# Attention layer of a four-layer graph kernel: one graph per step, scores in 32-row strips, maximum taken from PSUM and subtracted into SBUF

## The chip, the core and the metric

The kernel runs on one core of one Trainium2 chip. The metric is the device time of one execution in microseconds (us); the kernel before takes 859.26 us, the median of three runs (859.25 to 859.69). Engines are named TensorE (PE; its weight loads are PEld), VectorE (DVE), ScalarE (ACT), GpSimd (POOL) and SyncE (SP, here only transfers).

## What is computed

64 graphs of 128 nodes with 128 features go through four layers; each ends in `x = layernorm(layer(x) + x)`. Layer 2 (the third; they are counted from 0) is the one that changes: attention of 8 heads of width 16 in each graph, under the graph's adjacency.

```python
q = heads(x @ Wq.T + bq)
k = heads(x @ Wk.T + bk)
v = heads(x @ Wv.T + bv)
scores = jnp.einsum('bhnd,bhmd->bhnm', q, k) / math.sqrt(D)
...
```

Scores of absent edges are masked, a softmax runs over each row, its weights are multiplied with `v`, the heads are put side by side and multiplied with `Wo.T`, and `bo` is added. Layers 0 and 1 (a relational convolution and an attention of one head) come before it, layer 3 (additive attention, 8 heads) after it.

## The kernel before

`X` holds all 64 graphs in SBUF, 16 batches of `G` = 4 graphs. One layer runs over all batches before the next starts, and `later_layers` writes out the order of layers 1, 2 and 3 for each of PE, ACT and DVE; the few steps at a seam between layers are woven by hand (`layer2(BATCHES)` with `layer3(-1)`, for example). Every engine has its own program in this fixed order, and semaphores tie them; nothing is reordered by a scheduler. `need(eng, sem, v)` waits only if `v` is above zero.

Layer 2 works in units `u` of four heads of one graph, 8 units per batch, 128 in all. For one unit, on the engines:

- PE `layer2`: the mask (-1e30 for absent edges, bfloat16) goes into `bank[u % 2]` by a matmul with the identity (L1052), and the scores are added by one float32 matmul of 512 columns (L1054). Its moving operand `kexp` holds `k` once for each head with the other heads' rows at zero, so that the contraction over all 128 rows gives one head. POOL writes `kexp` in 8 operations per batch (L547, L550).
- DVE takes the negative maximum of each head from PSUM (L820, 512 elements per partition). ACT takes the exponential head by head, with that maximum as bias and the sum accumulated (L692, four operations and four reads of the accumulator). DVE takes the reciprocal (L851) and scales the weights in SBUF (L853).
- PE transposes the four 128x128 weights (L946, by `transposes`) into bank 2 or 3, ACT copies them (`copy_pT`, L667), PE multiplies them with `v` (`p_times_v`, L1039): four matmuls with 32 stationary columns, two heads in one group of 32 PSUM partitions, two groups. ACT copies the result (`copy_oT`, L676) and PE applies `Wo` (L1077).
- Once per batch come the transposes of the next `x`, the products for `k`, `q` and `v`, the adds of `bo` and `x`, the statistics and the norm.

Two units' scores stand in two banks in turn: while DVE and ACT work on one, PE fills the other. On PE a unit's scores stand ahead of the transposes of unit u-2 and the products of unit u-3. A float32 matmul appears as two matmul records (two passes) in the trace, a transpose as one.

`l3_weights` is DVE's preparation between layers 0 and 1, behind the flag (L316) that all engines branch on.

Of the kernel before, what the change touches and what calls it, by code (L numbers as in the profile page):

```python
# [11 lines left out]
F32 = mybir.dt.float32  # L12
BF16 = mybir.dt.bfloat16
# [35 lines left out]

def real(b):  # L50
    return not isinstance(b, int) or 0 <= b < BATCHES
# [10 lines left out]
def later_layers(eng, layer1, layer2, layer3, last):  # L62


    every_batch(eng, layer1, before=True, after=1)
    layer2(-1, 1, -1)
    layer1(BATCHES + 1, 1, BATCHES // 2)
    every_batch(eng, layer2)
    for u in range(UNITS):
        layer2(BATCHES, 0, BATCHES // 2, (u,))  # L70
        layer3(-1, 1, -1, (u,))
    layer2(BATCHES + 1, 1, BATCHES // 2)
    every_batch(eng, layer3, after=last)


def build(nc, t, out):
    ctx = ExitStack()
    with ctx:
# [10 lines left out]
        bank = [ctx.enter_context(nc.psum_tensor(f"bank{i}", [128, 512], F32)) for i in range(8)]  # L89
# [24 lines left out]
        qk_bias = sb("qk_bias", [128, 3])  # L114
        bv_row = sb("bv_row", [128, D])
# [54 lines left out]
        kT = sb("kT", [128, W])  # L170
        kexp = sb("kexp", [128, 2 * HEADS * W])
        adj = kexp[:].bitcast(I32)


        v2 = work
# [3 lines left out]
        den = [sb(f"den{i}", [128, HQ]) for i in range(4)]  # L179
        rd = [sb(f"rd{i}", [128, HQ]) for i in range(4)]  # L180
# [17 lines left out]
        def heads_of(mask, b, g):  # L198

            return mask[:, bass.ts(G * b + g, N)].unsqueeze(1).broadcast_to([128, HQ, N])  # L200

# [23 lines left out]
        add(oT_w[:], nat["L2_gnn_Wo"])  # L225
        add(bil[:], w1T[:], a12w[:], a12w_at)
        add(wa1[:], w1T[:], a_cols[:, 0:1].broadcast_to([128, 128]), w1_at)
# [32 lines left out]
        gsum = kexp[:, 0:GRAPHS * D]  # L260
# [57 lines left out]
        def general_dve(dve):  # L318
            def body(dve):
# [10 lines left out]
                def step(i, g, loop, r):  # L330
# [11 lines left out]
                    else:  # L342
                        nc.vector.tensor_tensor(ghg, bank[2][:], gbias, ALU.add).then_inc(sem("G_hg"), 1)
# [31 lines left out]
        def l3_weights(dve):  # L375
            dve.wait_ge(sem("params"), sems["n_params"])

# [127 lines left out]
        def _(pool):  # L505
# [31 lines left out]
            def layer1(b, s, turn):  # L537
                if isinstance(b, int) and b == BATCHES - 1:
                    layer2(-1, 1, -1)
                norm_pool(pool, 1, b, s, turn)  # L540

            def layer2(b, s, turn):
                if real(b + 1):
                    pool.wait_ge(sem("L2_k"), b + 2)
                    need(pool, sem("L2_s_mm"), UNITS * b)

                    nc.gpsimd.tensor_tensor(kexp[:, cols((1 - s) * HEADS, W)], kT[:],  # L547
                                            headmask[:, 0:1].broadcast_to([128, W]), ALU.mult)
                    for h in range(1, HEADS):
                        last = nc.gpsimd.tensor_scalar(kexp[:, cols((1 - s) * HEADS + h, W)], kT[:],  # L550
                                                       headmask[:, h:h + 1], 1.0, ALU.mult, ALU.mult)
                    last.then_inc(sem("L2_kexp"), 1)
                if real(b - 2):
                    norm_pool(pool, 2, b - 2, s, turn - 1)

            every_batch(pool, layer1)
            every_batch(pool, layer2, after=2)

            def layer3(b, s, turn):
                for u in range(UNITS):  # L560
                    if real(b):
# [14 lines left out]
        def _(act):  # L576
# [6 lines left out]
            for dst, src in ((nat["L0_gnn_W_loop"], t["L0_gnn_W_loop"][:, :]), (nat["L0_gnn_Wg_loop"], t["L0_gnn_Wg_loop"][:, :]),  # L583
# [6 lines left out]
                      (bv_row[:], row(t["L2_gnn_bv"], D)), (bo_row[:], row(t["L2_gnn_bo"], D)),  # L590
# [32 lines left out]
            def layer1(b, s, turn):  # L623
# [7 lines left out]
                if real(b):  # L631
# [3 lines left out]
                    nc.scalar.activation(uT[s], bank[1][:], ACT.Identity, bias=wa1[:, 0:1]).then_inc(sem("L1_uT"), 1)  # L635
# [508 lines left out]
```

## Time and profile before

| | |
|---|---|
| median of 3 runs | 859.26 us |
| the profiled execution | 859.89 us |
| its span (first to last instruction) | 858.2 us |
| PE busy | 781.1 us (91%) |
| DVE busy | 687.8 us (80%) |
| ACT busy | 642.2 us (75%) |
| POOL busy | 445.8 us (52%) |
| layer 2, first to last maximum (L820) | 229.1 to 572.1 us |
| layer 3, first mask matmul to the end | 583.8 to 858.2 us |

Busy time is the union of an engine's instructions; matmuls overlap in the pipeline, so PE's share says that it has work in flight, not that it runs at its peak. The span is the time from the first instruction to the last; about 1 us lies around it. Window rows further down give the busy time of each engine in a stretch, timeline rows give starts and durations.

### The profile page before, as it was taken

How to read it: one execution, taken by the hardware profiler on the slowest of the kernel's cores; microseconds unless marked ns; L12 is line 12 of the kernel's file. 1: busy time of each engine (PE TensorE's matmuls, PEld its weight loads, DVE VectorE, ACT ScalarE, POOL GpSimd, SP SyncE). 2: the span in 40 equal slices, each digit the busy share in tenths (PEclk: the TensorE clock that was granted, in tenths of full speed). 3: DMA queues.
4: the chain of work that ended last, by engine and by line, in shares of the span. 5: the costliest groups of instructions: out<-in, count | busy, mean ns of one | idle time of the engine just before them, and what ended most of it. 6: DMA issues, size and time to landing. Idle time of an engine off the chain costs nothing.

```text
span 858.2 us, 19137 instructions
## 1 busy us (share of the span) xinstructions
PE 781.1 (91%) x6059; PEld 527.3 (61%) x6059; DVE 687.8 (80%) x1919; ACT 642.2 (75%) x2116; POOL 445.8 (52%) x598
## 2 busy tenths in 40 slices
PE   3998899996699999999999999997999999999993
PEld 2776677775366666565666666555666666666652
DVE  3899288887577888888888888867899999999994
ACT  1544477777287777777777777776999999999993
POOL 4477233333533444444444444416567767767765
PEclk9999899999799999999999999998999999999998
DMA  8700000000000000000000000000000000000001
GB/s 247 205 2 1 2 1 2 1 2 1 1 1 1 2 1 2 2 1 2 2 2 1 1 1 2 2 1 1 2 14 14 27 15 14 27 14 14 26 14 38
DMA packets 28901, 15.09 MB, mean 18 GB/s; under 512 B 1792, under 2 KB 28800, under 8 KB 28800
## 3 DMA queue, kind: packets, MB, share of 16 engines
q1 hardware_dynamic: 25344, 12.59, 4.9%
q10 hardware_dynamic: 3456, 1.27, 0.6%
q8 instruction: 50, 0.82, 0.4%
q14 instruction: 51, 0.42, 0.2%
HBM read 9.65 MB, written 4.19 MB: 16 GB/s over the span
## 4 chain that ended last, share of the span: by engine, by line
PE 62%; DVE 17%; ACT 8%; issue 8%; POOL 2%; DMA 1%; DVEq 1%; POOLq 0%; ACTq 0%
PE bank L946 14%; PE bank L1054 12%; PE bank L1039 11%; PE bank L1052 5%; ACT loopm L640 3%; PE bank L1091 2%; DVE nmx L918 2%; DVE P L898 2%; PE bank L1094 2%; PE bank L1107 2%; DVE pT L804 2%; PE bank L1077 2%; PE bank L1012 2%; PE bank L1092 2%; PE bank L1006 2%
## 5 line engine op out<-in xcount | busy, mean ns | idle before, releaser
L692 ACT ACTIVATE P<-bank,nmx 128x128 f32<-128x128 f32 x512 | 181.3, 366 | 80.7 <-DVE nmx L820 80.5
L564 POOL TENSOR_TENSOR P<-P,nmx 128x512 f32<-128x512 f32 x128 | 133.2, 1041 | 80.5 <-DVE nmx L918 78.5
L946 PE MATMUL bank<-identf,P 128*128 128x128 f32 x1024 | 155.5, 274 | 1.6 <-DVE P L853 1.6
L667 ACT COPY pT<-bank 128x512 f32<-128x512 f32 x256 | 151.5, 593 | 0.4 <-PE bank L946 0.4
L820 DVE TENSOR_REDUCE nmx<-bank 128x4 f32<-128x512 f32 x128 | 88.3, 690 | 64.1 <-PE bank L1054 62.2
L459 POOL TENSOR_TENSOR ln<-ln,neghalf 128x4 f32<-128x4 f32 x64 | 66.2, 1034 | 138.6 <-DVE ln L495 138.6
L1054 PE MATMUL bank<-kexp,hg 128*128 128x512 f32 x256 | 132.3, 598 | 0.0
L946 PEld LDWEIGHTS bank<-identf,P 128*128 128x128 f32 x1024 | 113.9, 141 | 24.0 <-DVE P L853 14.2
L465 POOL TENSOR_SCALAR X<-yb,ln 128x128 f32<-128x128 f32 x256 | 119.4, 481 | 9.2 <-issue 9.2
L853 DVE TENSOR_TENSOR P<-P,rd 128x512 f32<-128x512 f32 x128 | 109.9, 859 | 4.4
L547 POOL TENSOR_TENSOR kexp<-kT,headmask 128x512 f32<-128x512 f32 x16 | 16.7, 1041 | 178.6 <-DVE kT L829 178.6
L898 DVE TENSOR_TENSOR P<-bank,t 128x512 f32<-128x512 f32 x128 | 87.5, 683 | 21.0 <-ACT t L707 20.8
L692 ACT ACTIVATION_READ_ACCUMULATOR P<-bank,nmx 128x1 f32 x512 | 103.9, 203 | 0.0
L550 POOL TENSOR_SCALAR kexp<-kT,headmask 128x512 f32<-128x512 f32 x112 | 102.8, 938 | 0.0
L707 ACT ACTIVATE t<-bank 128x512 f32<-128x512 f32 x128 | 77.7, 607 | 21.1 <-PE bank L1094 20.9
L918 DVE TENSOR_REDUCE nmx<-P 128x4 f32<-128x512 f32 x128 | 85.7, 670 | 0.8
L1039 PE MATMUL bank<-pT,work 128*32 128x128 f32 x1024 | 81.6, 279 | 1.7 <-ACT oT L676 0.9
L711 ACT ACTIVATE P<-P 128x512 f32<-128x512 f32 x128 | 80.9, 632 | 2.2 <-POOL P L564 2.2
L1039 PEld LDWEIGHTS bank<-pT,work 128*32 128x32 f32 x1024 | 47.4, 109 | 23.4 <-issue 21.0
L486 DVE BATCH_NORM_STATS2 bn<-yb 128x6 f32<-128x128 f32 x256 | 60.8, 281 | 1.2
L1094 PEld LDWEIGHTS bank<-eT,sel 128*128 128x128 bf16 x512 | 39.8, 99 | 31.1 <-issue 1.6
L1039 PE MATMUL bank<-pT,vx 128*32 128x128 f32 x1024 | 54.5, 285 | 2.0 <-ACT pT L667 1.8
(158 smaller groups left out, 1504.3 us busy)
## 6 DMA issues: line engine op xcount, KB each, us to landing
X<-in_x SPq DMA_DIRECT2D x16, 256.0 KB, 5.4
kexp<-in_adj SPq DMA_DIRECT2D x16, 256.0 KB, 5.3
out<-X SPq DMA_DIRECT2D x16, 256.0 KB, 2.3
nat_all<-in_L_gnn_W ACTq DMA_DIRECT2D x2, 64.0 KB, 4.1
w<-in_L_gnn_W ACTq DMA_DIRECT2D x2, 64.0 KB, 4.6
nat_all<-in_L_gnn_W_loop ACTq DMA_DIRECT2D x1, 64.0 KB, 2.7
nat_all<-in_L_gnn_Wg_loop ACTq DMA_DIRECT2D x1, 64.0 KB, 3.3
hg_bias<-in_L_gnn_b_loop ACTq DMA_DIRECT2D x1, 64.0 KB, 5.1
```

What stands on the lines that cost most here:

```text
L465: last = nc.gpsimd.tensor_scalar(x_of(b)[:, cols(g)], yb[s][:, cols(g)], ln[s][:, g:g + 1], ln[s][:, 2 * G + g:2 * G + g + 1], ALU.add, AL ...
L550: last = nc.gpsimd.tensor_scalar(kexp[:, cols((1 - s) * HEADS + h, W)], kT[:], headmask[:, h:h + 1], 1.0, ALU.mult, ALU.mult)
L564: nc.gpsimd.tensor_tensor(v3(P[u % 4][:], HQ), v3(P[u % 4][:], HQ), nmx[u % 4][:].unsqueeze(2).broadcast_to([128, HQ, N]), ALU.add)\
L667: nc.scalar.copy(pT[uu % 2][:], bank[2 + uu % 2][:]).then_inc(sem(f"L{L}_pT"), 1)
L692: last = nc.scalar.activation(P[u % 4][:, cols(j)], bank[u % 2][:, cols(j)], ACT.Exp, bias=nmx[u % 4][:, j:j + 1], accum_out=den[u % 4][:, ...
L820: nc.vector.tensor_reduce(nmx[u % 4][:], v3(bank[u % 2][:], HQ), AX.X, ALU.max, negate=True)\
L853: nc.vector.tensor_tensor(v3(P[uu % 4][:], HQ), v3(P[uu % 4][:], HQ), rd[uu % 4][:].unsqueeze(2).broadcast_to([128, HQ, N]), ALU.mult)\
L898: nc.vector.tensor_tensor(P[u % 4][:], bank[u % 2][:], t3[u % 2][:], ALU.max)\
L918: nc.vector.tensor_reduce(nmx[u % 4][:], v3(P[u % 4][:], HQ), AX.X, ALU.max, negate=True)\
L946: last = nc.tensor.transpose(dst[:, cols(i)], src[:, cols(i)], identf[:])
L1039: last = mm(bank[6][row:row + HP, cols(col)], (v2 if L == 2 else vx)[ss][:, cols(HEADS * g + h, HP)], pT[uu % 2][:, cols(j)], start=start, ...
L1054: mm(bank[u % 2][:], qT[s][:, cols(g)], kh, start=False, stop=True).then_inc(sem("L2_s_mm"), 1)
```

## The change

Layer 2 is written anew as a step `t` per graph (64 steps, and 16 that drain), with all 8 heads at once:

- `pair[0]` is banks 0 and 1 as one PSUM tensor of 1024 columns, `pair[1]` banks 2 and 3. One graph's scores take the whole of `pair[0]`, and there is no second buffer for them: PE's mask matmuls of graph t wait for `L2_less_max` of graph t-1.
- `kexp` and POOL's writes of it are gone. ACT writes `kk`: for even and odd heads, `k` with the other half's rows at zero. A strip is a matmul whose operands are 32 rows of `qT` and `kk` (two heads), 256 columns wide. Strips 0 and 1 go to banks 0 and 1, then come the 8 transposes of graph t-2, then strips 2 and 3, again to banks 0 and 1.
- DVE takes the maximum over 1024 columns from PSUM and then adds its negative to the scores, from PSUM into `P2` in SBUF. ACT takes one exponential of 1024 columns there. The sum of a row is no longer accumulated: `v` is held as `vx`, 32 columns a head with a column of ones, so the product gives the sum as well. The 8 products of a graph go to four groups of 32 partitions (`HP * (h % 4)`).
- Their result is transposed back (2 transposes per graph), scaled by the reciprocal of the sum into `on` (DVE), per batch transposed again (`onT`), multiplied with `Wo`, with `bo` added by a bfloat16 matmul of three parts. `bv` and the parts of `bo` are prepared in `l3_weights` and one more `prep` product.
- ACT copies `xT` and writes `k` and `q`. The norm is split over POOL's steps. The first two units of layer 3 wait for the last residual of layer 2 (`L2_y_done`).

```diff
     every_batch(eng, layer1, before=True, after=1)
-    layer2(-1, 1, -1)
+    for t in range(-4, 0):
+        layer2(t)
     layer1(BATCHES + 1, 1, BATCHES // 2)
-    every_batch(eng, layer2)
+    for t in range(GRAPHS):
+        layer2(t)
     for u in range(UNITS):
-        layer2(BATCHES, 0, BATCHES // 2, (u,))
+        layer2(GRAPHS + u)
         layer3(-1, 1, -1, (u,))
...
         def l3_weights(dve):
             dve.wait_ge(sem("params"), sems["n_params"])
+            dve.wait_ge(sem("pool_ready"), 1)
+            nc.vector.tensor_reduce(evenodd[:], headmask[:].rearrange("p (a b) -> p b a", b=2), AX.X, ALU.add)\
+              .then_inc(sem("kmask_set"), 1)
+            nc.vector.memset(bo3[:], 0.0).then_inc(sem("bo_set"), 1)
...
+            nc.vector.tensor_tensor(bo2[:], bvo[:], bo_row[:], ALU.add).then_inc(sem("bo_set"), 1)
+            for part in range(3):
...
+                nc.vector.tensor_copy(bo_part[:], bo2[:]).then_inc(sem("bo_set"), 1)
...
+                nc.vector.tensor_copy(v3(bo3[at, :], G), bo_part[at, :].unsqueeze(1).broadcast_to([1, G, D]))
+                nc.vector.tensor_tensor(bo2[:], bo2[:], bo_part[:], ALU.subtract).then_inc(sem("bo_set"), 1)
```

ScalarE, per step: `k` of the next batch, the copy of the transposed weights, the exponential, the copy of the product:

```diff
+                if j == 1 and real(b + 1):
+                    act.wait_ge(sem("L2_k_mm"), b + 2)
...
+                    for e in range(2):
+                        last = nc.scalar.activation(k[:, e], v3(bank[5], G), ACT.Identity, bias=bk2[:, e:e + 1],
+                                                    scale=evenodd[:, e:e + 1])
...
+                if graph(t - 2):
+                    act.wait_ge(sem("L2_pT_mm"), t - 1)
+                    need(act, sem("L2_pv_mm"), t - 3)
+                    nc.scalar.copy(pT2[t % 2], pair[1][:]).then_inc(sem("L2_pT"), 1)
+                if graph(t - 1):
+                    act.wait_ge(sem("L2_less_max"), t)
+                    p = P2[(t - 1) % 3]
+                    nc.scalar.activation(p, p, ACT.Exp).then_inc(sem("L2_exp"), 1)
+                if graph(t - 3):
...
+                    nc.scalar.copy(oT[(t - 3) % 2][:], bank[6][:, 0:2 * N]).then_inc(sem("L2_oT"), 1)
```

VectorE:

```diff
+                if graph(g):
+                    dve.wait_ge(sem("L2_out_mm"), g + 1)
+                    nc.vector.reciprocal(rd3[g % 2][:], o[:, :, HD]).then_inc(sem("L2_rden"), 1)
...
+                if graph(t):
+                    dve.wait_ge(sem("L2_s_mm"), 2 * (t + 1))
+                    need(dve, sem("L2_pT_mm"), t - 2)
+                    nc.vector.tensor_reduce(nmx2[t % 2][:], v3(pair[0][:], HEADS), AX.X, ALU.max, negate=True)\
+                      .then_inc(sem("L2_max"), 1)
+                    dve.wait_ge(sem("L2_max"), t + 1)
+                    nc.vector.tensor_tensor(v3(P2[t % 3], HEADS), v3(pair[0][:], HEADS),
+                                            nmx2[t % 2][:].unsqueeze(2).broadcast_to([128, HEADS, N]), ALU.add)\
+                      .then_inc(sem("L2_less_max"), 1)
```

TensorE, up to the last strips:

```diff
+                def strips(first):
+                    for i in range(first, first + 2):
+                        rows = slice(HP * i, HP * i + HP)
+                        last = mm(bank[i % 2][:, cols(i // 2, 2 * N)], qT[s][rows, cols(j)], kk[s][rows, cols(j, 2 * N)],
+                                  start=False, stop=i >= 2)
...
+                if graph(t):
...
+                    need(pe, sem("L2_less_max"), t)
+                    for i in range(2):
+                        mm(bank[i], identb[:], heads_of(mask2, b, j), start=True, stop=False)
+                    strips(0)
+                if graph(t - 2):
+                    pe.wait_ge(sem("L2_exp"), t - 1)
+                    need_or(pe, sem("L2_pT"), t - 2, sem("L1_xw"), BATCHES)
+                    for i in range(2):
+                        last = transposes(bank[2 + i], P2[(t - 2) % 3][:, cols(i, W)], HQ)
+                    last.then_inc(sem("L2_pT_mm"), 1)
+                if graph(t):
+                    pe.wait_ge(sem("L2_s01_mm"), 2 * (t + 1))
+                    strips(2)
```

TensorE, layer 3:

```diff
                         need(pe, sem("L3_leaky"), U - 1)
...
+                        if U < 2:
+                            pe.wait_ge(sem("L2_y_done"), BATCHES)
```

On PE in the middle of layer 2, one graph was two units; these rows are one unit and the start of the next, before (`bank`, `kexp`, `hg`: scores from `kexp` and `qT`; `identf,P`: transposes; `pT,work`: products with `v`):

```order
L1052 MATMUL bank<-mask,identb 128x512 [waits L2_exp]
L1054 MATMUL bank<-kexp,hg 128x512
L1077 MATMUL bank<-oT_w,oT 128x128 [waits L2_oT]
L946 MATMUL bank<-identf,P 128x128 [waits L2_pT,L2_p]
L946 MATMUL bank<-identf,P 128x128 x3
L1039 MATMUL bank<-pT,work 32x128 [waits L2_pT]
L1039 MATMUL bank<-pT,work 32x128 x3
```

The same place after the change, one whole graph with the batch's transposes of `x` and products for `v` (`arena,hg`: strips of `kk` and `qT`; `identf,arena`: transposes of `P2`; `arena,vx`: products with `v`):

```order
L1064 MATMUL pair<-mask,identb 128x512 [waits L2_less_max,L2_q,L2_k]
L1055 MATMUL pair<-arena,hg 128x256 x2
L979 MATMUL pair<-identf,arena 128x128 [waits L2_pT,L2_exp]
L979 MATMUL pair<-identf,arena 128x128 x7
L1055 MATMUL pair<-arena,hg 128x256 [waits L2_s01_mm]
L1055 MATMUL pair<-arena,hg 128x256
L1082 MATMUL bank<-arena,vx 32x128 [waits L2_oT,L2_pT]
L1082 MATMUL bank<-arena,vx 32x128 x7
L979 MATMUL bank<-identf,oT 128x128 [waits L2_on,L2_oT]
L979 MATMUL bank<-identf,X 128x128 [waits L2_xT,L2_y_done,L1_norm_done]
L1099 MATMUL bank<-vT_w,xT 128x128 [waits L2_q]
```

The first score matmul waited for the exponential of two units earlier, and now waits for the subtraction of the graph just before; the transposes stand between the strips.

On DVE the same stretch before, a unit's maximum, a copy for the batch, and the reciprocal and scaling of the unit ahead:

```order
L820 TENSOR_REDUCE nmx<-bank 128x4 [waits L2_exp,L2_s_mm]
L825 COPY xT<-bank 128x512 [waits L2_v_mm,L2_xT_mm]
L851 RECIPROCAL rd<-den 128x4 [waits L2_exp]
L853 TENSOR_TENSOR P<-P,rd 128x512 [waits L2_rden]
```

And after, one graph, with the batch's copy of `onT` (`hg`):

```order
L869 RECIPROCAL rd<-bank 128x8 [waits L2_out_mm]
L878 COPY hg<-bank 128x512 [waits L2_o_mm,L2_onT_mm]
L887 TENSOR_TENSOR arena<-bank,rd 128x128 [waits L2_rden]
L893 TENSOR_REDUCE nmx<-pair 128x8 [waits L2_pT_mm,L2_s_mm]
L896 TENSOR_TENSOR arena<-pair,nmx 128x1024 [waits L2_max]
```

All four rows stood there twice per graph (the copy once per batch). The scaling moved from the weights to the product, and a pass of the width of the scores came in behind the maximum.

On DVE between the flag and the first operation of layer 1 these now stand ahead of the old preparation (`bo` stands for `bo2` and `bo3`):

```order
L403 TENSOR_REDUCE evenodd<-headmask 128x2 [waits pool_ready,params]
L407 TENSOR_SCALAR bk<-evenodd,qk_bias 128x2 [waits kmask_set]
L413 CAST bo_part<-bo 128x128 [waits bo_set]
L415 COPY bo<-bo_part 1x512 [waits bo_set]
L416 TENSOR_TENSOR bo<-bo,bo_part 128x128
L419 TENSOR_TENSOR a_prod<-nat_all,a_row 128x128 x2
```

The last three of the new ones come three times; `a_prod` was first before.

## Rows read from the trace of the kernel before

**Rows 1.** The page: its span, and the granted clock in 40 slices.

```profile
span 858.2 us, 19137 instructions
...
PEclk9999899999799999999999999998999999999998
```

**Rows 2.** Windows, layers 2 and 3: busy PE, PEld, DVE, ACT, POOL; then the granted clock.

```profile
583.80:858.20 274.40, 248.97 (x2672) 165.95 (x2672) 239.65 (x673) 239.35 (x508) 185.51 (x215) 0.98 0.06 17
229.10:572.10 343.00, 339.95 (x2238) 205.20 (x2238) 274.70 (x614) 269.74 (x1217) 151.35 (x192) 1.00 0.01 1
```

**Rows 3.** Line L820: ns minimum/median/maximum, first and last start in us.

```profile
L820 DVE TENSOR_REDUCE nmx<-bank x128: 676/692/694, 229.1 to 572.1; 128x4 f32<-128x512 f32 x128
```

**Rows 4.** Waits in layer 2: who waited for whom, us in total, times, longest.

```profile
DVE nmx L820 <- PE bank L1054: 61.8, 94, 3.1
...
PEld bank L946 <- DVE P L853: 14.2, 20, 2.4
```

**Rows 5.** Timeline of PE through one unit of layer 2: start, duration, instructions.

```profile
429.46 0.60 PE L946 MATMUL bank<-identf,P 128*128 128x128 f32 x4
429.99 0.64 PE L1039 MATMUL bank<-pT,work 128*32 128x128 f32 x8
430.56 0.39 PE L1052 MATMUL bank<-mask,identb 128*128 128x512 bf16 x1
430.79 0.59 PE L1054 MATMUL bank<-kexp,hg 128*128 128x512 f32 x1
```

**Rows 6.** Timeline of layer 2: DVE to DVE, DVE to PE, PE to DVE.

```profile
233.26 0.17 DVE L851 RECIPROCAL rd<-den 128x4 f32<-128x4 f32 x1
...
233.46 0.69 DVE L853 TENSOR_TENSOR P<-P,rd 128x512 f32<-128x512 f32 x1
...
234.20 0.33 PE L946 MATMUL bank<-identf,P 128*128 128x128 f32 x1 [1.55 <-DVE P L853]
...
433.83 1.02 PE L1054 MATMUL bank<-kexp,hg 128*128 128x512 f32 x2
...
434.89 0.69 DVE L820 TENSOR_REDUCE nmx<-bank 128x4 f32<-128x512 f32 x1 [0.76 <-PE bank L1054]
```

**Rows 7.** Timeline of layer 3: the products with `v`, four heads in four groups.

```profile
701.69 0.43 PE L1039 MATMUL bank<-pT,vx 128*32 128x128 f32 x8
```

**Rows 8.** Groups by line: count, busy us, mean ns, idle time before them.

```profile
L763 DVE TENSOR_TENSOR vals<-bank,hg 128x256 f32<-128x256 f32 x32 | 11.9, 414 | 7.5 <-ACT hg L609 7.5
L898 DVE TENSOR_TENSOR P<-bank,t 128x512 f32<-128x512 f32 x128 | 87.5, 683 | 21.0 <-ACT t L707 20.8
L667 ACT COPY pT<-bank 128x512 f32<-128x512 f32 x256 | 151.5, 593 | 0.4 <-PE bank L946 0.4
L711 ACT ACTIVATE P<-P 128x512 f32<-128x512 f32 x128 | 80.9, 632 | 2.2 <-POOL P L564 2.2
L748 DVE COPY bias<-bias_part 1x256 bf16<-1x256 bf16 x6 | 1.3, 297 | 0.1
L379 DVE TENSOR_TENSOR a_prod<-nat_all,a_row 128x128 f32<-128x128 f32 x2 | 0.5, 277 | 0.0
```

**Rows 9.** Timeline, layer 0 to layer 1: the end of `l3_weights` and DVE's next operation.

```profile
90.26 0.16 DVE L387 COPY wh_w<-a_sum 128x8 f32<-128x8 f32 x1
...
91.43 0.69 DVE L795 COPY xT<-bank 128x512 f32<-128x512 f32 x1 [1.01 <-PE bank L946]
```

**Rows 10.** Timeline, layer 1 to layer 2.

```profile
220.02 1.16 PE L1069 MATMUL bank<-vT_w,xT 128*128 128x128 f32 x8
...
221.97 1.00 DVE L784 SCALAR_TENSOR_TENSOR elu<-pT,elu 128x512 f32<-128x512 f32 x1 [2.01 <-ACT elu L630]
...
226.78 0.59 PE L1052 MATMUL bank<-mask,identb 128*128 128x512 bf16 x1 [5.60 <-POOL kexp L550]
```

**Rows 11.** Timeline, layer 2 to layer 3: the last maximum and the first mask of layer 3.

```profile
572.05 0.69 DVE L820 TENSOR_REDUCE nmx<-bank 128x4 f32<-128x512 f32 x1 [0.35 <-PE bank L1054]
...
583.79 0.61 PE L1091 MATMUL bank<-mask,identb 128*128 128x512 bf16 x1 [0.68 <-ACT eT L702]
```

More of the change, by code:

```diff
@@ L47, in need_or, with graph @@
         eng.wait_ge(sem, value)
+HEAD_AT = (0, 1, 4, 5, 2, 3, 6, 7)
+def graph(t):
+    return 0 <= t < GRAPHS
 def real(b):
@@ L87, in sem @@
             return sems[name]
-        bank = [ctx.enter_context(nc.psum_tensor(f"bank{i}", [128, 512], F32)) for i in range(8)]
+        pair = [ctx.enter_context(nc.psum_tensor(f"pair{i}", [128, 1024], F32)) for i in range(2)]
+        bank = [pair[i // 2][:, i % 2 * 512:i % 2 * 512 + 512] for i in range(4)]
+        bank += [ctx.enter_context(nc.psum_tensor(f"bank{i}", [128, 512], F32))[:] for i in range(4, 8)]
         def cols(i, n=D):
@@ L169, in build @@
         qT = [uT[s] for s in range(2)]
[L170 to L175, printed above, removed]
+        arena = sb("arena", [128, 16 * W])
+        adj = arena[:].bitcast(I32)
+        P2 = [arena[:, cols(i, 2 * W)] for i in range(3)]
+        pT2 = [arena[:, cols(3 + i, 2 * W)] for i in range(2)]
+        kk = [arena[:, cols(5 + i, 2 * W)] for i in range(2)]
+        on = [arena[:, cols(14 + i, W)] for i in range(2)]
+        onT = y2[0]
         vx = [sb(f"vx{s}", [128, G * HEADS * HP]) for s in range(2)]
@@ L200, in heads_of, with out_bank @@
             return mask[:, bass.ts(G * b + g, N)].unsqueeze(1).broadcast_to([128, HQ, N])
+        def out_bank(b):
+            return bank[4] if b < BATCHES - 2 else bank[1]
         prep = []
@@ L537, in layer1, with layer2 @@
             def layer1(b, s, turn):
-                if isinstance(b, int) and b == BATCHES - 1:
-                    layer2(-1, 1, -1)
                 norm_pool(pool, 1, b, s, turn)
[L542 to L554, printed above, removed]
+            def layer2(t):
+                b, j = t // G - 3, t % G
+                if j == 3 and real(b):
+                    norm_pow(pool, 2, b, b % 2, b // 2)
+                    norm_scale(2, b, b % 2, (0, 1))
+                if j == 0 and real(b - 1):
+                    norm_scale(2, b - 1, (b - 1) % 2, (2, 3))
             every_batch(pool, layer1)
-            every_batch(pool, layer2, after=2)
+            for t in range(GRAPHS + UNITS):
+                layer2(t)
             def layer3(b, s, turn):
                 for u in range(UNITS):
+                    if b == 0:
+                        layer2(GRAPHS + UNITS + u)
                     if real(b):
@@ L1082, in layer3 @@
+                        row, col = HP * j, 2 * (g % 2) + hq
+                        last = mm(bank[6][row:row + HP, cols(col)], vx[ss][:, cols(HEADS * g + h, HP)],
+                                  pT[uu % 2][:, cols(j)], start=True, stop=True)
+                    last.then_inc(sem(f"L{L}_pv_mm"), 1)
             def layer3(b, s, turn, units=range(UNITS)):
```

314 lines of the change are left out of this document (156 added, 158 removed).

## The prediction

> **What bounds the kernel now.** First the page: the span is 858.2 us, and the granted clock is high nearly throughout, with dips near the seams between layers [rows 1]. Then the windows: in layer 2, PE has work in flight in 339.95 of 343.00 us at clock 1.00, while DVE is busy 274.70 and ACT 269.74 [rows 2]. The waits agree: DVE waits 61.8 us for PE's scores, PE waits 14.2 us for DVE's scaled weights, nearly all of it at the start, and almost nothing else [rows 4]. So layer 2 is bound by PE's stream. Its period is (572.1 - 229.1) / 127 = 2.70 us per unit, 5.40 per graph [rows 3]. Whoever shortens PE's stream and keeps two score buffers gains; this change shortens the stream but gives the second buffer up. So the question is no longer how much work PE has, but how long one turn of the loop mask, strips, maximum, subtraction, next mask takes.
>
> **The step of PE.** Unit rows give starts, and the differences are what an item costs in a full stream [rows 5]. Four transposes and the change to the 32-column products: 429.99 - 429.46 = 0.53. A transpose in the stream is 0.11 (0.60 for four, of which 0.27 is the pipeline of the last), so 0.09 is a pause at the change of shape. The eight passes of the products and the pause behind them take 430.56 - 429.99 = 0.57. A mask matmul takes 0.23, and a float32 matmul of 512 columns 0.86 in two passes of 0.43 (its two records span 1.02, 0.17 beyond the stream [rows 6]), so a pass of 256 columns takes 0.21.
>
> Do matmuls in different parts of the array overlap? For column groups, yes: eight passes over two groups span 0.64 [rows 5], eight over four groups 0.43 [rows 7]; four rounds became two. For row groups no row shows it. Bounds for a pair of strips: fully side by side 2 x 0.21 = 0.43, in a row 0.86. I take side by side, since the column rows are the nearest and the two strips write different banks. The first weights after a pause are not hidden: eight passes of a 128-column float32 product span 1.16 after idle time [rows 10], where 7 x 0.11 + 0.28 = 1.05 would do; so 0.10 for each pair of strips, and 0.05 before transposes (0.33 for the first one after a wait [rows 6], 0.28 in the stream).
>
> From the first mask to the end of the last strip: masks 0.44; pause 0.09; strips 0 and 1 0.54; pause 0.09; eight transposes 0.05 + 0.87; pause 0.09; strips 2 and 3 0.54, and 0.17 until the result is there. Sum 2.88.
>
> The rows show a pause of 0.09 at each change of shape. The Trainium skill (TensorEngine Tiling, Key Properties) says that changing the tiling mode drains the engine; the trace agrees, for column shapes. For row tiles it gives (TensorE: Matmul & The Clock Gate, Measured speedup vs the span model) 3.07 times for four of 512 columns, the only figure for what no row here shows; by it a pair would be nearly side by side, as in my sum.
>
> **The step of DVE.** A two-operand pass from PSUM takes 414 ns for 256 columns and 683 for 512 [rows 8], so 1.05 ns a column; 1024 take 1.22. The maximum takes 0.69 for 512 [rows 3], by the same slope 1.23. DVE starts 0.04 after the scores' end (433.83 + 1.02 to 434.89), 0.03 lie between dependent operations, and PE starts 0.05 after DVE's end (233.46 + 0.69 to 234.20) [rows 6]. Together 0.04 + 1.23 + 0.03 + 1.22 + 0.05 = 2.57.
>
> **The loop** takes 2.88 + 2.57 = 5.45 us per graph. What else must fit beside it? PE behind the last strip: products 0.09 + 0.46, two transposes 0.36 with pause, and per step one of: `x` transposes and `v` 1.33, `k` and `onT` 1.30, `q` 0.86, `bo` and `Wo` 1.10. That ends by 2.71 + 0.91 + 1.33 = 4.95, under 5.45: hidden, with 0.5 to spare. DVE's reciprocal, scaling and one copy (0.2 + 0.3 + 0.7, and two statistics 0.5) lie beside PE's 2.88. ACT has a copy of 1024 (0.59 + 0.42), an exponential (0.63 + 0.42), a copy of 0.40 and at most two passes of 0.7: 3.9 us. All are covered; each costs nothing as long as the loop stays above 4.95. POOL's `kexp` goes, but it was not on the path except at the first batch.
>
> So PE's load per graph does fall (about 4.7 against 5.40), and none of that is seen, because the loop's 5.45 takes its place. 63 x 5.45 = 343.4 against 343.0: **+0.4**. The rows show DVE's two passes as 2.57 of 5.45. The Trainium skill (TensorEngine Tiling, PSUM Bottleneck) warns that tiling speeds up the engine and not the way out of PSUM; by it, as by the rows, the gain of the strips stays unpaid here.
>
> **The seams.** Layer 0 to 1: 12 more operations on DVE, of 0.15 to 0.3 each (a_prod 277 ns, a one-row copy of 256 elements 297 ns, so some 0.5 for 512 [rows 8]), three rounds of a chain of three, about 1.0 each, and 0.6 ahead of them. DVE stood 1.01 us between its last preparation and the copy [rows 9], and part of that is the branch on the flag, which stays; so nearly all of 3.6 shows: **+3.5** (bounds 2.5 and 5).
>
> Layer 1 to 2: PE stood 5.60 us for `kexp` [rows 10]. ACT's `k` (2 x 0.7) comes instead, then `q` must wait for it since both use bank 5. In rows 10 `v` starts at 220.02 behind `q`, so `k`'s product is there at about 219.1; 219.1 + 1.4 + 1.0 for `q` + 0.7 on ACT gives the first mask at about 222.2 instead of 226.78. But DVE's tail of layer 1 now hides nothing: ACT begins that tail behind `q`, at 222.2 instead of 220.7, and DVE's part starts at 223.5 instead of 221.97. It takes 3.2 instead of 4.1 without POOL beside it (1.00 for a pass that takes 0.69 elsewhere). So the first maximum comes at 226.8 instead of 229.1: **-2.3**. PE then waits some 3 us for the first subtraction, so the next steps run at the lower clock: **+1.5** (0 to 3).
>
> Layer 2 to 3: before, 583.79 - 572.05 = 11.7 us from last maximum to first mask of layer 3 [rows 11]. Now: maximum and subtraction 2.5; exponential behind a copy 2.6; transposes 1.1; copy 1.05; products 0.8; copy 0.45; back transposes 0.35; `Wo` of batch 14 with its residual 2.0; scaling 0.3; `onT` 0.6 and copy 0.75; `bo` and `Wo` 1.3; residual 0.7, for which layer 3's first mask waits. Sum 14.5: **+2.8** (0 to 5). Statistics and norm of the last batch now lie in layer 3's first units: **+0.5**.
>
> Sum: 0.4 + 3.5 - 2.3 + 1.5 + 2.8 + 0.5 = +6.4, so a span of 864.6. The profiled execution's own time (859.89) lies 0.6 above the median and its span 1.1 below the median; from the median, **865.7 us**.
>
> **Rivals.**
> 1. *The strips don't overlap.* For it: no row shows row groups side by side. Against: rows 5 and 7 show column groups so, and the banks differ. Each pair costs 0.43 more: 63 x 0.86 = +54, 920 us. If only their weight loads queue up, about half a pass per pair, 63 x 0.22 = +14, 880.
> 2. *The other side: the strips need no pause.* If the array takes row strips between full matmuls without a pause and loads their weights ahead, three pauses (0.27) and the exposed loads (0.25) go: the loop is 4.93, and PE's own stream, 4.4 to 4.7, nearly binds too. 63 x (4.93 - 5.45) = -33: 833 us. It decides for faster from a loop under 5.35, that is if 0.10 goes per graph. For it: half of PE's changes of shape in the old stream cost nothing visible (bfloat16 mask to float32 scores), but those are all full-sized. Against: every change to or from a part of the array costs 0.09 or more in rows 5.
> 3. *The early weights only.* One exposed load is hidden or one pass is shorter than I take it: loop 5.3, -9.5, 856 us.
> 4. *The clock.* PE stands 0.5 us per step; layer 3 stands more (busy 248.97 of 274.40) and keeps 0.98 [rows 2]. So I give it little; at the lower clock the loop would gain over 2 us.
>
> **Chances.** Forecast with its neighbourhood (858 to 874) 0.52; rival 1 in full 0.11, in part 0.11; rival 2 0.13; rival 3 0.11; clock 0.02. The range should leave out full rival 1 and the clock and reaches to the others: 832 to 884. Measurement tells 0.2% (1.7 us) from no change. Faster (below 857.5): rivals 2 and 3 and a little of the neighbourhood, 0.29; same 0.09; slower 0.62.
>
> **What would show it.** Start to start of L893 (maximum) should be 5.45 in mid-stage; the strips' four records should start in two close pairs, 0.21 apart, some 0.1 late after masks and transposes (in rival 1, four starts 0.21 apart). L893 and L896 should take 1.22 to 1.23 each. PE's mask L1064 should wait for DVE L896 in nearly every step, about 0.5 us; if it doesn't, PE's stream binds and the working of the pauses is wrong. The first L893 should stand 1 us or so later than 229.1 (+3.5 - 2.3), the first mask of layer 3 at about 588. The prediction fails if a pair of strips takes clearly other than 0.54, or if DVE or ACT holds the loop at a place that I call covered.

## The result, and the profile after

The kernel after takes **885.10 us** (median of four runs, 881.33 to 888.53) beside 859.44 of the kernel before (859.25 to 859.69). The ratio is 1.0297, with a 95% interval of 1.0252 to 1.0342: slower by 3%. The prediction had the sign and the loop that sets the step of layer 2, but a quarter of the size: +6.4 us where +25.7 came, and 885.1 lies just outside its range of 832 to 884. What failed most is its term for the lower clock of TensorE: it had +1.5 us, and layer 2 lost 10.8.

The page of the profiled execution (886.5 us), its busy line, the granted clock in 40 slices and the three groups that make the loop:

```profile
span 884.7 us, 18573 instructions
...
PE 769.3 (87%) x6525; PEld 519.9 (59%) x6525; DVE 636.1 (72%) x1754; ACT 554.1 (63%) x1141; POOL 325.3 (37%) x470
...
PEclk9999899998659999999999999979999999999998
...
L893 DVE TENSOR_REDUCE nmx<-pair 128x8 f32<-128x1024 f32 x64 | 78.4, 1225 | 135.4 <-PE pair L1055 135.4
...
L896 DVE TENSOR_TENSOR arena<-pair,nmx 128x1024 f32<-128x1024 f32 x64 | 78.4, 1224 | 2.2
...
L1064 PE MATMUL pair<-mask,identb 128*128 128x512 bf16 x128 | 40.7, 401 | 40.4 <-DVE arena L896 39.4
```

Every engine has less to do than before, and the program is longer: DVE stands 135.4 us before the maximum, waiting for the strips, and PE stands 40.4 us before the mask, nearly all of it for DVE's subtraction. That is a loop of two engines in turn. The clock row has a dip to 6 and 5 in slices 11 and 12 (7 and 9 in rows 1 of the kernel before), where layer 2 begins, and one to 7 in slice 27, where it ends (before, 8 in slice 28).

Windows of the kernel after (stretch, its length; busy PE, PEld, DVE, ACT, POOL; granted clock, DMA share, GB/s). The last row is the middle of layer 2, to be held against the second of [rows 2]:

```profile
240.10:264.00 23.90, 21.60 (x100) 12.28 (x100) 8.35 (x9) 7.92 (x10) 0.00 (x0) 0.50 0.00 1
264.00:281.00 17.00, 13.62 (x117) 7.07 (x114) 8.57 (x12) 8.82 (x12) 0.00 (x0) 1.00 0.01 1
281.00:284.50 3.50, 3.50 (x24) 2.48 (x28) 0.49 (x1) 1.68 (x2) 0.00 (x0) 0.51 0.00 0
...
584.80:595.10 10.30, 10.27 (x52) 7.25 (x53) 4.83 (x15) 2.34 (x3) 2.74 (x5) 0.50 0.01 3
286.00:584.00 298.00, 267.07 (x2326) 162.27 (x2324) 190.31 (x382) 154.23 (x214) 32.86 (x60) 1.00 0.01 1
```

PE had work in flight in 339.95 of 343.00 us; now in 267.07 of 298.00, at full clock. It stands a tenth of the time. And 37.7 us of layer 2 and its end (23.9 + 3.5 + 10.3) ran at 0.50, the lower level of 1.2 GHz.

The waits of the kernel after from 286 to 584 us (engine, line, waited for: us in total, times, longest), which answer to [rows 4]:

```profile
DVE nmx L893 <- PE pair L1055: 103.1, 54, 2.6
...
PEld pair L1064 <- DVE arena L896: 38.2, 41, 1.6
...
PE pair L1064 <- DVE arena L896: 30.0, 53, 1.2
```

**Where the 26.5 us of span went.** Five marks in both timelines divide it:

| stretch | before | after | more | forecast |
|---|---|---|---|---|
| start to the first maximum of layer 2 | 229.11 | 231.46 | +2.4 | +1.2 |
| first to last maximum | 342.94 | 358.67 | +15.7 | +1.9 |
| last maximum to the first mask of layer 3 | 11.74 | 19.17 | +7.4 | +2.8 |
| that mask to the end | 274.37 | 275.39 | +1.0 | +0.5 |

The step of the loop, taken from the starts of L893 in mid-stage, is 5.50, 5.50, 5.51 and 5.58 within a batch, 5.523 on average. 63 steps of it are 347.9, that is +5.0 against before; the other 10.8 of the 15.7 are steps that ran at the lower clock (up to 7.92 us each).

### The profile page after: what moved, and what is told of

It reads as the page before. It is cut to its first block, busy times and chain, and to the rows that moved or that the text cites. A ratio compares the mean times of both kernels' runs of the same rounds, so it can differ in the third digit from the quotient of the medians.

```text
span 884.7 us, 18573 instructions
## 1 busy us (share of the span) xinstructions
PE 769.3 (87%) x6525; PEld 519.9 (59%) x6525; DVE 636.1 (72%) x1754; ACT 554.1 (63%) x1141; POOL 325.3 (37%) x470
## 4 chain that ended last, share of the span: by engine, by line
PE 47%; DVE 33%; issue 8%; ACT 7%; POOL 2%; DVEq 1%; DMA 1%; POOLq 1%; ACTq 0%
PE pair L979 11%; PE pair L1055 10%; DVE arena L896 9%; DVE nmx L893 9%; PE pair L1064 4%; PE bank L979 4%; ACT loopm L675 3%; PE bank L1145 2%; PE pair L1160 2%; DVE nmx L951 2%; DVE P L931 2%; PE pair L1163 2%; PE bank L1045 2%; PE pair L1161 2%; DVE pT L853 2%
## 5 line engine op out<-in xcount | busy, mean ns | idle before, releaser
L893 DVE TENSOR_REDUCE nmx<-pair 128x8 f32<-128x1024 f32 x64 | 78.4, 1225 | 135.4 <-PE pair L1055 135.4
L736 ACT COPY arena<-pair 128x1024 f32<-128x1024 f32 x64 | 64.8, 1012 | 172.1 <-PE pair L979 172.1
L931 DVE TENSOR_TENSOR P<-pair,t 128x512 f32<-128x512 f32 x128 | 87.5, 684 | 22.4 <-ACT t L756 20.5
L1055 PE MATMUL pair<-arena,hg 32*128 32x256 f32 x512 | 95.2, 449 | 0.2
L756 ACT ACTIVATE t<-pair 128x512 f32<-128x512 f32 x128 | 77.4, 605 | 22.9 <-PE pair L1163 22.6
L896 DVE TENSOR_TENSOR arena<-pair,nmx 128x1024 f32<-128x1024 f32 x64 | 78.4, 1224 | 2.2
L979 PE MATMUL pair<-identf,P 128*128 128x128 f32 x512 | 78.2, 275 | 0.0
L979 PE MATMUL pair<-identf,arena 128*128 128x128 f32 x520 | 75.9, 292 | 1.7 <-DVE arena L887 1.0
L1064 PE MATMUL pair<-mask,identb 128*128 128x512 bf16 x128 | 40.7, 401 | 40.4 <-DVE arena L896 39.4
L702 ACT COPY pT<-pair 128x512 f32<-128x512 f32 x128 | 74.8, 585 | 0.4 <-PE pair L979 0.4
L740 ACT ACTIVATE arena<-arena 128x1024 f32<-128x1024 f32 x64 | 67.9, 1061 | 1.5 <-DVE arena L896 1.5
L1055 PEld LDWEIGHTS pair<-arena,hg 32*128 32x128 f32 x512 | 40.5, 193 | 41.7 <-issue 40.4
```

The lines of the kernel that those rows point to most:

```text
L702: nc.scalar.copy(pT[uu % 2][:], bank[2 + uu % 2]).then_inc(sem(f"L{L}_pT"), 1)
L756: nc.scalar.mul(t3[u % 2][:], bank[u % 2], ALPHA).then_inc(sem("L3_scaled"), 1)
L893: nc.vector.tensor_reduce(nmx2[t % 2][:], v3(pair[0][:], HEADS), AX.X, ALU.max, negate=True)\
L896: nc.vector.tensor_tensor(v3(P2[t % 3], HEADS), v3(pair[0][:], HEADS), nmx2[t % 2][:].unsqueeze(2).broadcast_to([128, HEADS, N]), ALU.add)\
L931: nc.vector.tensor_tensor(P[u % 4][:], bank[u % 2], t3[u % 2][:], ALU.max)\
L979: last = nc.tensor.transpose(dst[:, cols(i)], src[:, cols(i)], identf[:])
```

## Experiments

Each kernel ran four times, the first four kernels on one chip beside the kernel before (859.9 us, seven runs), the last four on another beside it (859.68, seven runs). Ratios are to the kernel before on the same chip.

**x_order: the transposes behind all strips.** The loop is shortened by what stood inside it for no reason of data.

```diff
                     strips(0)
+                if graph(t):
+                    pe.wait_ge(sem("L2_s01_mm"), 2 * (t + 1))
+                    strips(2)
                 if graph(t - 2):
                     ...
                     last.then_inc(sem("L2_pT_mm"), 1)
-                if graph(t):
-                    pe.wait_ge(sem("L2_s01_mm"), 2 * (t + 1))
-                    strips(2)
```

> The changed kernel with the eight transposes of graph t-2 moved behind strips 2 and 3, so that they no longer stand between the mask and the last strip. Theory A (the loop mask, strips, maximum, subtraction binds layer 2, 5.50 us per graph): the loop loses 8 x 0.11 and one pause with its exposed load and gains a short wait for strips 0 and 1, so it falls to about 4.65, and PE's own stream of 4.95 takes over: 63 x 0.55 = 35 us less, about 850, and fewer stretches at the lower clock since PE stands less. Theory B (PE's stream binds already, or DVE and ACT do): within 5 us of 885.

Measured: **838.07** (837.23 to 839.89), ratio 0.9748, interval 0.9722 to 0.9774. That is 47 us under the kernel after, and 2.5% under the kernel before. One step of it in the timeline (start, duration, instructions, idle time before and for whom):

```profile
447.42 0.59 PE L1064 MATMUL pair<-mask,identb 128*128 128x512 bf16 x2
...
447.95 1.50 PE L1055 MATMUL pair<-arena,hg 32*128 32x256 f32 x8
...
449.38 1.09 PE L979 MATMUL pair<-identf,arena 128*128 128x128 f32 x8
449.52 1.23 DVE L893 TENSOR_REDUCE nmx<-pair 128x8 f32<-128x1024 f32 x1 [1.00 <-PE pair L1055]
...
450.78 1.22 DVE L896 TENSOR_TENSOR arena<-pair,nmx 128x1024 f32<-128x1024 f32 x1
...
452.58 0.59 PE L1064 MATMUL pair<-mask,identb 128*128 128x512 bf16 x2
```

The middle of its layer 2 as a window (columns as above):

```profile
262.00:540.00 278.00, 271.13 (x2412) 169.59 (x2425) 202.12 (x391) 157.55 (x222) 32.88 (x60) 1.00 0.01 1
```

And its waits in the same stretch (from 262 to 540 us: total, times, longest):

```profile
PEld pair L1064 <- DVE arena L896: 9.0, 15, 0.6
```

The transposes (449.38) now lie beside the maximum instead of ahead of it. The mask of the next graph follows 0.58 us after DVE's end (450.78 + 1.22 = 452.00), so in this step the loop no longer binds; PE is busy again in 271.13 of 278.00. The steps of a batch are 5.15, 5.12, 4.68 and 4.93, on average 0.55 under 5.52. That is 35 us, to about 850 as expected. From first to last maximum it takes 310.8 us where the kernel after took 358.7, 47.9 less: besides those 35, the 10.8 of the clock, which in this kernel is low near layer 2 only from 218.5 to 222 and from 225.3 to 235.5, and about 2 for the light steps at both ends, which take 4.64 to 4.72. The same matmuls, the same bytes, the same banks: what made the kernel after slow was the length of its loop and what followed from it.

**x_halfmax: DVE's part of the loop cut by a half pass.** The maximum runs over the four heads of bank 0 alone and serves both banks, so half the maxima are left out; everything else stays.

```diff
-                    nc.vector.tensor_reduce(nmx2[t % 2][:], v3(pair[0][:], HEADS), AX.X, ALU.max, negate=True)\
+                    nc.vector.tensor_reduce(nmx2[t % 2][:, 0:HQ], v3(bank[0], HQ), AX.X, ALU.max, negate=True)\
```

> The changed kernel with the maximum taken over the four heads of bank 0 only, and used for the heads of bank 1 as well (the maximum of the other four heads is left out). PE's work is untouched, DVE's maximum takes 0.69 instead of 1.23. Theory A (the loop binds): 0.54 less per graph, the period falls to about 4.97, close to PE's own stream; 63 x 0.53 = 33 us less, about 850. Theory B (PE's stream binds, and the shorter one of DVE's passes is covered): 885.

Measured: 843.09 (837.96 to 848.42), ratio 0.982, interval 0.9755 to 0.9884. DVE in its timeline, two steps:

```profile
440.28 0.69 DVE L893 TENSOR_REDUCE nmx<-pair 128x4 f32<-128x512 f32 x1 [1.77 <-PE pair L1056]
441.00 1.22 DVE L896 TENSOR_TENSOR arena<-pair,nmx 128x1024 f32<-128x1024 f32 x1
...
445.25 0.69 DVE L893 TENSOR_REDUCE nmx<-pair 128x4 f32<-128x512 f32 x1 [1.79 <-PE pair L1056]
```

The pass is 0.53 shorter (1.22 to 0.69) and so is the step (5.50 to 4.97). A loop passes on the whole of what one member saves. 63 x 0.53 = 33. In the profiled execution (837.96 us) first to last maximum takes 313.7, 45.0 less than in the kernel after; the rest is nearly all the 10.8 of the clock, since layer 2 ran at 1.00 throughout from 233.4 to 545.1 us. The four runs lie in two pairs, 838 at a mean granted clock of 0.978 and 848 at 0.964: time and clock go together over 10 us in one and the same program. The median, 42 us under the kernel after, lies between the pairs.

**x_prep: the new preparations out of the first seam.** The thirteen operations that the change put into `l3_weights` (the prediction counted twelve) run at the start of DVE's `layer2(-4)`, where DVE waits anyway.

> The changed kernel with the twelve new preparations on DVE (parts of bo, even and odd bk) moved from the place between flag and layer 1 to DVE's idle time between layers 1 and 2 (7.9 us). Theory A (they delay layer 1 one to one): 3.3 us less, 881 to 882. Rival: layer 1 or the seam behind it takes the delay up, less than 1 us.

Measured: 881.21 (878.99 to 884.9), ratio 1.0256, interval 1.0224 to 1.0289; 3.9 under the kernel after. The runs of the two kernels overlap (the kernel after has 881.33 to 888.53), so it is the timeline that shows the effect: the first copy of `xT` of layer 1 starts at 91.44 (before 91.43, after 94.70), so the +3.3 of that seam are those operations, and the first maximum comes at 227.52. This run had another use: its seam from layer 2 to 3 ran at full clock throughout and took 16.76 us (16.75 in x_halfmax, at full clock too). So of that seam's +7.4, +5.0 is its chain and +2.4 the clock.

**x_fill: more work for PE in the light steps.** After steps -4 to -2, 0 to 3, 5 to 7 and 61 to 63, PE does 3 to 16 bfloat16 matmuls of 256 columns whose results nobody uses; after steps -4 and 61 it first waits until the bank is free.

```diff
+            FILL = {-4: (6, 4), -3: (6, 8), -2: (6, 4), 0: (6, 12), 1: (6, 16), 2: (6, 12), 3: (7, 16),
+                    5: (4, 8), 6: (4, 3), 7: (4, 13), 61: (5, 10), 62: (5, 10), 63: (5, 4)}
...
+                for _ in range(n):
+                    mm(bank[at][:, 2 * N:4 * N], identb[:], mask1[:, 0:2 * N], start=True, stop=True)
```

> The changed kernel with idle-time matmuls on PE (bfloat16 identity times 256 mask columns into a bank that is free there, results unused) in the light steps: steps -4 to 3, 5 to 7 and 61 to 63, 4 to 16 in each. Theory C (the 10.8 us over 5.5 per step in layer 2 are the lower granted clock, which falls where PE stands in light steps): the clock returns near 236 us and stays, steps 2 to 8 and 63 take 5.5, 8 to 12 us less, 873 to 877, and the runs spread less. Rival D (those steps are long for want of filled pipelines, not for the clock): no gain, and some us more for the added work.

Measured: **874.38** (873.61 to 875.49), ratio 1.0167, interval 1.0141 to 1.0192. More work makes the kernel 10.7 us faster, and its runs lie within 1.9 us of each other instead of 7.2. The early maxima in DVE's timeline of the kernel after:

```profile
236.10 1.22 DVE L893 TENSOR_REDUCE nmx<-pair 128x8 f32<-128x1024 f32 x1 [1.57 <-PE pair L1055]
242.74 1.22 DVE L893 TENSOR_REDUCE nmx<-pair 128x8 f32<-128x1024 f32 x1 [4.16 <-PE pair L1055]
250.60 1.22 DVE L893 TENSOR_REDUCE nmx<-pair 128x8 f32<-128x1024 f32 x1 [5.38 <-PE pair L1055]
258.52 1.22 DVE L893 TENSOR_REDUCE nmx<-pair 128x8 f32<-128x1024 f32 x1 [5.44 <-PE pair L1055]
```

And in that of x_fill:

```profile
242.38 1.22 DVE L893 TENSOR_REDUCE nmx<-pair 128x8 f32<-128x1024 f32 x1 [4.24 <-PE pair L1069]
247.88 1.23 DVE L893 TENSOR_REDUCE nmx<-pair 128x8 f32<-128x1024 f32 x1 [3.02 <-PE pair L1069]
253.46 1.23 DVE L893 TENSOR_REDUCE nmx<-pair 128x8 f32<-128x1024 f32 x1 [3.10 <-PE pair L1069]
```

In the kernel after, up to 7.92 us apart at clock 0.50; with the filling, 5.50 and 5.58, as in mid-stage. From 238.0 us to the last maximum at 579.4 the clock is 1.00, and first to last maximum takes 348.8, where 63 steps of mid-stage are 347.9. So 9.9 us of the table's second row went with the low clock, and more work for PE in its light steps was enough for that. All those steps were filled at once; which of them matter was not tried.

**y_order_prep: both edits that keep the result.** x_order and x_prep together.

> x_order and x_prep together: transposes behind all strips, DVE's new preparations in its idle time after layer 1. If the two costs lie at different places they add: 838.1 - 3.9, about 834, 25 us under the kernel before. Rival: they share something (the state of the clock at the seam), then 836 to 838.

Measured: 837.17 (831.59 to 839.66), ratio 0.9746, interval 0.9721 to 0.9771. The profiled execution has a span of 829.9 against 835.4 of x_order, but the medians differ by 0.9 only: its runs follow their granted clock (831.59 at 0.982, 839.66 at 0.970). Whether the 3.3 us add to x_order's gain stays open. What the clock does ahead of layer 2 differs by more than that: x_order's profiled execution has a mean clock of 0.53 from 92 to 103 us, while this one runs at 1.00 from 92 to 98, and at a mean of 0.53 from 209 to 231. This version and x_order can't be told apart; both are 2.5% under the kernel before and compute everything.

**y_order_halfmax: does the loop bind anywhere any more?** x_order and x_halfmax together.

> x_order with the maximum over the heads of bank 0 only (the other four heads' maximum is left out). In x_order the steps of a batch take 5.15, 5.12, 4.68, 4.93. Theory A: the first two and the last are PE's own stream, only the third is the loop (4.65), so 0.54 off DVE's part of the loop gives under 0.1 in one step of four: 0 to 2 us less than 838. Rival: the loop binds still, 9 us (one step in four) to 34 us (all) less.

Measured: 834.15 (832.78 to 838.62), ratio 0.9714, interval 0.9677 to 0.975; 3.9 under x_order, which is more than the 0 to 2 of theory A and far less than the 9 of the rival. The steps in mid-stage are 5.15, 5.12, 4.68 and 4.93, as without the cut pass; only the light steps at both ends shrink (4.11), and first to last maximum takes 307.4 instead of 310.8. Those light steps, in which the loop still binds, are 3.5 of the 3.9 us, and theory A left them out. The half pass that was worth 0.53 per step in the kernel after is worth nothing in mid-stage here. There all four steps of x_order are PE's own stream, the one of 4.68 too, which looked like the loop.

**y_seam: an earlier start of layer 3.** On top of y_order_prep, the first unit of layer 3 doesn't wait for the last residual of layer 2, only the second does.

```diff
-                        if U < 2:
+                        if U == 1:
                             pe.wait_ge(sem("L2_y_done"), BATCHES)
```

> y_order_prep where only the second unit of layer 3, which writes bank 1, waits for the last residual of layer 2, no longer the first one. If that wait sets the start of layer 3, its first unit starts about 1 us earlier and the whole gains up to 1 us; if the second unit's wait or DVE's order holds it anyway, less than 0.5.

Measured: 839.26 (831.26 to 840.41), ratio 0.973, interval 0.9678 to 0.9781. Inconclusive in time: the seam took 19.3 us with two stretches of lower clock in it, against 18.0 at full clock in y_order_prep, and the runs spread over 9 us, which is more than the edit could bring. The trace shows that the edit does what it should: the first mask of layer 3 starts at 562.55, ahead of the last residual at 562.79, where in y_order_prep it starts 0.84 behind that residual's start. DVE's first addition of layer 3, counted from the same residual, comes 0.46 earlier.

**y_order_prep_fill: the filling where PE's stream binds.** y_order_prep with the matmuls of x_fill.

> y_order_prep with the idle-time matmuls of x_fill. Theory C (lower clock follows standing in light steps): with the shorter loop PE stands so little that the clock stays high without them, so no gain, within 1.5 us of y_order_prep, where the same matmuls gave 10 us to the changed kernel. Rival: they gain as before, 5 us or more.

Measured: 839.26 (837.3 to 840.49), ratio 0.9758, interval 0.9733 to 0.9783. No gain over y_order_prep, but 2.1 us more, where theory C had 1.5 at most: seven of the first eight steps are longer (5.01 to 5.85, against 4.64 to 5.06), since the added work now lies on PE, which sets the step, while in x_fill it lay in PE's idle time. First to last maximum takes 315.8 instead of 310.9. The mean granted clock of the runs is higher than without the filling (0.980 to 0.989 here, 0.970 to 0.982 in y_order_prep). So the filling doesn't pay here, but the run doesn't show that the clock had no need of it.

## Why the prediction was right and where it was not

One step of the kernel after in mid-stage, PE and DVE (start, duration, instructions, idle time before), to be laid beside the prediction's working of 2.88 + 2.57:

```profile
441.24 0.60 PE L1064 MATMUL pair<-mask,identb 128*128 128x512 bf16 x2 [0.34 <-DVE arena L896]
441.77 0.70 PE L1055 MATMUL pair<-arena,hg 32*128 32x256 f32 x4
442.40 1.09 PE L979 MATMUL pair<-identf,arena 128*128 128x128 f32 x8
443.43 0.70 PE L1055 MATMUL pair<-arena,hg 32*128 32x256 f32 x4
...
444.20 1.23 DVE L893 TENSOR_REDUCE nmx<-pair 128x8 f32<-128x1024 f32 x1 [1.77 <-PE pair L1055]
...
445.46 1.23 DVE L896 TENSOR_TENSOR arena<-pair,nmx 128x1024 f32<-128x1024 f32 x1
...
446.74 0.60 PE L1064 MATMUL pair<-mask,identb 128*128 128x512 bf16 x2 [0.37 <-DVE arena L896]
```

**What bounds the kernel: right.** With the transposes inside the loop, the second score buffer was worth more than the work that PE saves. L1064 waits for L896 in nearly every step, as the last part of the prediction asked.

**The loop: 5.45 forecast, 5.50 to 5.58 measured.** By parts: masks and pause 0.53 (forecast 0.53); strips 0 and 1 with pause 0.63 (0.63); transposes with pause 1.03 (1.01); strips 2 and 3 to their result 0.70 (0.71); DVE's start 0.07 (0.04); two passes with what lies between 2.49 (2.48); PE's start 0.05 (0.05). All terms held within 0.03. The strips do overlap: four passes of 256 columns span 0.70, where four in a row at 0.21 with their end would take about 1.1, so rival 1 is out in full and in part, and the pauses and exposed weights are there, so rivals 2 and 3 are out. Yet the mean step of 5.523 is 0.073 over the forecast, and 63 x 0.073 = 4.6 us: a term that is repeated 63 times wants a third digit, and 5.45 stood nearer to the old 5.40 than its working was sure.

**PE's own stream: forecast 4.4 to 4.95, at most; measured 4.68 to 5.15** where it binds (x_order). The wait of strips 2 and 3 for 0 and 1, with nothing between them, is in those steps: 1.43 from the first strip to the transposes, where two pairs with pause take 1.26 in the kernel after. That the stream was hidden in the kernel after was right.

**Layer 0 to 1: right** (+3.3 for +3.5, though for thirteen operations and not twelve), and x_prep shows the cause. The kernel after:

```profile
93.65 0.16 DVE L427 COPY wh_w<-a_sum 128x8 f32<-128x8 f32 x1
...
94.70 0.69 DVE L844 COPY xT<-pair 128x512 f32<-128x512 f32 x1 [0.89 <-issue]
```

The end of the preparations moved from 90.26 [rows 9] by 3.4, and the copy behind it by as much.

**Layer 1 to 2: the sign was right, the size not** (-2.3 forecast; the first maximum is +2.4 over before with +3.3 inherited, so -0.9):

```profile
227.31 1.01 PE L1064 MATMUL pair<-mask,identb 128*128 128x512 bf16 x2 [0.87 <-ACT hg L731]
...
228.38 0.69 DVE L833 SCALAR_TENSOR_TENSOR elu<-pT,elu 128x512 f32<-128x512 f32 x1 [7.91 <-ACT elu L665]
```

PE's wait for `kexp`, 5.60 us in [rows 10], has gone as forecast. But the clock is low here from 216.2 to 233.3 (before, in two shorter stretches from 213.5 to 230.6): the two masks span 1.01 instead of 0.60, and the products for `k` and `q` take 2.07 and 2.08 instead of about 1.0, which the sum had at full speed. DVE's tail of layer 1 sets the first maximum, as the sum had it: 3.08 from L833 to the maximum (3.2 forecast).

**The clock: the step that failed.** The sum had +1.5 for lower clock, for the first steps only, and the fourth rival dismissed more with "layer 3 stands more and keeps 0.98". An average over a long layer says nothing of its ends. The reason given for the +1.5 was wrong too: PE did not stand 3 us for the first subtraction but 0.50 (ahead of the mask at 233.99), since the transposes of `x` and the products for `v` lay between, and the clock was 1.00 from 233.3 to the fall at 240.1.

The clock fell at 240.1, at 281.0 and at 584.8 us. What PE did before: steps 0 to 7 lack the work of the drained stages (no `onT`, `bo` and `Wo` yet), steps from 61 on lack `x`, `v`, `k` and `q` of a next batch, and the loop keeps each at 5.5 us all the same; so PE stood up to some 2 us at a time. In the old kernel PE's own stream set the pace, a light step was simply shorter, and PE stood little (3.1 of 341.5 us from 230.6 to 572.1). Once low, the clock stayed low for 24 us although PE had matmuls in flight in 21.60 of 23.90, for at half speed the same work fills the step. x_fill shows that the light steps are the cause: the same loop, PE given work in its idle time, 10.7 us less.

The Trainium skill (TensorE: Matmul & The Clock Gate, HAM oscillation) tells of this swing for a matmul kernel that waits for DMA, and lays it to long idle gaps. The trace here agrees on the swing and not on the gaps: none ahead of these three falls is longer than about 2 us (1.56, 1.76 and 1.67 before the masks there). PE of the kernel after ahead of the first two falls, at 240.1 and 281.0:

```profile
238.64 0.60 PE L1064 MATMUL pair<-mask,identb 128*128 128x512 bf16 x2 [1.56 <-DVE arena L896]
...
279.77 0.59 PE L1064 MATMUL pair<-mask,identb 128*128 128x512 bf16 x2 [1.76 <-DVE arena L896]
```

And of x_order, where the clock was 1.00 from 235.5 on and stayed there:

```profile
239.79 0.61 PE L1064 MATMUL pair<-mask,identb 128*128 128x512 bf16 x2 [1.56 <-DVE arena L896]
```

The kernel before has such a wait too (1.55 in rows 6) at full clock. So the length of one wait doesn't decide whether the clock falls; what does is not shown.

The last fall cost the seam 2.4 us. PE there, with the first mask of layer 3 at the end:

```profile
584.83 1.02 PE L1064 MATMUL pair<-mask,identb 128*128 128x512 bf16 x2 [1.67 <-DVE arena L896]
...
593.61 1.78 PE L979 MATMUL pair<-identf,arena 128*128 128x128 f32 x8
```

Eight transposes span 1.78 where they take 1.09 at full clock.

**Layer 2 to 3: the chain was too short** (14.5 forecast, 16.76 at full clock in x_prep, 19.17 here). PE in the timeline of the kernel after:

```profile
599.76 0.66 PE L1176 MATMUL bank<-wh_w,xT 128*128 128x144 f32 x4
600.35 0.64 PE L1082 MATMUL bank<-arena,vx 128*32 128x128 f32 x16
```

DVE behind it:

```profile
601.94 0.29 DVE L914 COPY er<-bank 128x32 f32<-128x32 f32 x2 [0.30 <-PE bank L1176]
...
602.37 0.29 DVE L887 TENSOR_TENSOR arena<-bank,rd 128x128 f32<-128x128 f32 x1
```

PE again, the last back transposes and the first mask of layer 3:

```profile
602.81 0.41 PE L979 MATMUL bank<-identf,oT 128*128 128x128 f32 x2 [0.91 <-DVE arena L887]
...
609.30 0.38 PE L1160 MATMUL pair<-mask,identb 128*128 128x512 bf16 x1 [0.88 <-DVE yb L882]
```

From the last back transposes (602.81) to the mask the terms of the sum hold: scaling, `onT`, copy, `bo` and `Wo`, residual and the residual of batch 14 gave 5.65, and 5.94 lie between 603.22 and the end of the last residual at 609.16. The excess lies ahead of them. Layer 3's preparation is woven in there: its products L1176 stand on PE ahead of the last products with `v`, and its copy L914 stands on DVE ahead of the scaling L887 for which the back transposes wait 0.91. In numbers: the products end 1.40 after the copy of the weights (600.99, 599.59), where the sum had 0.8, and the back transposes 1.79 after the copy of the product (603.22, 601.43), where it had 0.35. These 2.0 us, less 0.2 for an exponential that came sooner (in x_prep), and 0.3 in the part behind are the 2.2. The sum followed layer 2's own chain and left out what the neighbouring layer queues between its links; that is read from the timeline and was not tried by an edit.

Sum of the misses: 4.6 for the loop, about 9.3 for the clock in layer 2 (10.8 for 1.5), 1.4 at layer 1 to 2, 2.2 for the chain and 2.4 for the clock at layer 2 to 3, 0.5 in layer 3, less 0.2 at layer 0 to 1: 20.2, and 26.5 - 6.4 = 20.1. So the clock is more than half of the miss.

## What to carry to other kernels

Before a double buffer is given up, write down one whole turn of the loop that then arises and ask of every item in it whether the data need it there: eight transposes that only stood between two pairs of strips made the difference between 3% slower and 2.5% faster. A loop that paces two engines also takes the speed-up out of light steps at the ends of a stage, and there the clock of a TensorE that then stands can fall; read the clock at the ends of a stage, not its mean over the layer. At a seam, the chain has to be followed through everything that stands in each engine's queue, the next layer's preparations too.

## What the runs showed of the hardware

- Float32 matmuls over 32 rows and 256 columns in two different row groups and banks run side by side: four passes (two strips of two) span 0.70 us. A change between full matmuls and strips costs about 0.09 (two masks to the first strip 0.53, of which the masks are 0.44), as it does for column groups [rows 5], and the next pair of strips into the same banks, when it must wait for the first, 0.17 more (1.43 in x_order for 1.26).
- The granted clock can stay at 0.50 for 24 us with matmuls in flight 90% of the time (21.60 of 23.90), and it fell without any gap longer than about 2 us ahead of it. It stayed at 1.00 behind gaps of 1.55 and 1.56 in the kernel before and in x_order, so one gap's length doesn't decide it. Adding matmuls that nobody uses gained 10.7 us and cut the spread of the runs from 7.2 to 1.9 us.
- The time of one program follows its clock from run to run: 888.53 at a mean of 0.954, 886.5 at 0.958, 883.7 at 0.962, 881.33 at 0.968.
- A DVE pass over 1024 float32 columns of PSUM takes 1.22 us over two banks, as a maximum and as an addition alike, as the slope of shorter ones had given.
